# A four-layer kernel: softmax, sigmoid and one Silu written with Tanh, and a power by squarings on GpSimd

## The reference, cut to what matters

```
# conditioning of layer 1: each sequence has one expert of 8
expert = argmax(opcode_onehot, -1)
hidden = silu(x @ W_up[expert].T) * (x @ W_gate[expert].T)        # 256 wide
out = hidden @ W_down[expert].T

# feed-forward of layer 1: the two best of 8 experts for each token
gate_scores = softmax(x @ Wg + bg)                                # over 8 experts
topk_scores, topk_idx = top_k(gate_scores, 2)
top_probs = softmax(topk_scores)                                  # over the two
out = sum over the two of top_probs * (relu(x W1 + b1) W2 + b2)

# feed-forward of layer 2: again the two best of 8, routed by a sigmoid
probs = sigmoid(x @ router_w.T + routing_bias)
topk_p, topk_idx = top_k(probs, 2); topk_p /= sum(topk_p)
out = shared SwiGLU(x) + sum over the two of topk_p * (silu(x wg) * (x wu)) wd
```

## Time and profile before

| what | value |
|---|---|
| median of three runs | 1442.39 us (1441.62 to 1445.08) |
| the profiled execution | 1442.76 us, its span 1440.9 us |
| granted TensorE clock, mean of the span | 0.96 |
| PE, DVE, ACT, POOL busy | 1248.3, 856.1, 710.7, 269.1 us |
| instructions in the trace | 26352 |

### The profile page before, as it was taken

How to read it: one execution, slowest core, us unless ns; L and a number is a source line. 1 busy time by engine, 2 the same in 40 slices (tenths; PEclk the granted TensorE clock), 3 DMA queues, 4 the chain that set the end, 5 groups by cost and what they waited for, 6 DMA issues and landing times.

```text
span 1440.9 us, 26352 instructions
## 1 busy us (share of the span) xinstructions
PE 1248.3 (87%) x9301; PEld 967.7 (67%) x9301; DVE 856.1 (59%) x1800; ACT 710.7 (49%) x1385; POOL 269.1 (19%) x454
## 2 busy tenths in 40 slices
PE   4799960678988889998988999989999998998989
PEld 2455620346877779887777888589888854456867
DVE  4878669654445466657776445466564566664242
ACT  1556668545445434444444445333434376665554
POOL 1899200000001213330000003043320111100000
PEclk9899985799999999999999999999999999999999
DMA  8000010211050213212205200123120000000000
GB/s 304 1 2 2 2 73 0 116 81 59 1 198 10 90 56 102 56 29 96 110 1 210 88 1 25 48 80 88 36 94 1 1 1 2 2 2 1 0 15 15
DMA packets 42607, 75.71 MB, mean 53 GB/s; under 512 B 3817, under 2 KB 33521, under 8 KB 41585
## 3 DMA queue, kind: packets, MB, share of 16 engines
q1 hardware_dynamic: 38384, 65.62, 12.5%
q0 software_dynamic: 4096, 8.40, 2.0%
HBM read 59.72 MB, written 14.29 MB: 51 GB/s over the span
## 4 chain that ended last, share of the span: by engine, by line
PE 67%; DVE 15%; ACT 9%; issue 5%; POOL 2%; DVEq 1%; DMA 1%; ACTq 0%; SPq 0%; POOLq 0%
PE bank L1635 7%; PE bank L1624 7%; PE bank L1620 6%; PE bank L1679 5%; PE bank L1413 3%; PE bank L1479 3%; PE bank L1689 3%; PE bank L1611 3%; PE bank L1418 3%; PE bank L1420 2%; PE bank L1419 2%; PE bank L1604 2%; PE bank L1606 2%; PE bank L1605 2%; PE bank L1529 2%
## 5 line engine op out<-in xcount | busy, mean ns | idle before, releaser
L1872 ACT ACTIVATE SC<-bank 128x512 f32<-128x512 f32 x192 | 114.1, 596 | 220.4 <-PE bank L1620 130.3
L1959 DVE SCALAR_TENSOR_TENSOR SC<-bank,SM,SC 128x512 f32<-128x512 f32 x128 | 95.9, 749 | 142.6 <-PE bank L1624 119.7
L2549 POOL DMA_INDIRECT xs<-CC,POSI x64 | 63.6, 994 | 536.1 <-DVE POSI L2353 234.0
L1635 PE MATMUL bank<-A,SC 128*128 x1024 | 137.1, 277 | 10.5 <-DVE SC L1959 9.6
L1624 PE MATMUL bank<-X,SC 128*128 128x128 f32 x1024 | 137.3, 277 | 6.1 <-DVE SC L2234 5.8
L1620 PE MATMUL bank<-X,SC 128*128 128x128 f32 x1024 | 137.5, 278 | 2.0 <-ACT SC L1856 2.0
L1635 PEld LDWEIGHTS bank<-A,SC 128*128 128x128 f32 x1024 | 125.4, 192 | 20.2 <-issue 19.4
L1620 PEld LDWEIGHTS bank<-X,SC 128*128 128x128 f32 x1024 | 128.5, 195 | 14.4 <-issue 12.5
L1624 PEld LDWEIGHTS bank<-X,SC 128*128 128x128 f32 x1024 | 125.4, 193 | 8.2 <-DVE SC L2234 8.1
L1679 PE MATMUL bank<-A 128*128 128x128 f32 x736 | 99.6, 279 | 11.8 <-DVE A L2374 8.1
L1772 ACT ACTIVATE A<-bank,SM 128x128 f32<-128x128 f32 x256 | 73.6, 383 | 66.0 <-DVE SM L2055 65.7
(11 more groups left out here) (319 smaller groups left out, 2570.3 us busy)
## 6 DMA issues: line engine op xcount, KB each, us to landing
A<-in_moe SPq DMA_DIRECT2D x36, 768.0 KB, 10.2
A<-xs SPq DMA_DIRECT2D x20, 256.0 KB, 3.4
ys<-A SPq DMA_DIRECT2D x20, 256.0 KB, 2.4
BW<-in_l1f SPq DMA_DIRECT2D x2, 2048.0 KB, 7.8
BW<-in_l2f SPq DMA_DIRECT2D x1, 3456.0 KB, 12.0
BW<-in_l1c SPq DMA_DIRECT2D x1, 3072.0 KB, 17.0
BW<-in_l3f SPq DMA_DIRECT2D x1, 2816.0 KB, 9.5
A<-in_l1c SPq DMA_DIRECT2D x1, 2560.0 KB, 8.6
```

The source lines that it names most:

```text
L1635: m = e.matmul(o, at["h"].ap[:, cut(q)], W[:, bass.ds(r + (1024 + 128 * q), 128)], start=k == 0 and q == 0, stop=k == 1 and q == 3)
L1872: e.activation(at["h"].ap, at["pg"].ap, ACT.Gelu_apprx_tanh).then_inc(at["gelu"][0], 1)
L1959: return e.scalar_tensor_tensor(out=o, in0=a, scalar=s, in1=b, op0=o1, op1=o2)
```

## The change

The three functions are written with Tanh. For the conditioning, silu(u) * g = 0.5 * ((1 + tanh(u/2)) * u) * g: ACT does Tanh with scale 0.5, and DVE's one product becomes two that depend on each other, with a wait between them. For the routing, (1 + tanh(x/32)) / (1 - tanh(x/32)) is exp(x/16), and four squarings make exp(x) of it (for L = 1 exp(-x), so that 1 / (1 + it) is the sigmoid; the sign that DVE's form leaves is lost in the squarings). DVE makes the fraction with three instructions, POOL does the four squarings, and this is a step of its own, `r_pow`, and a stage of its own: `r_top` and `r_hot` come one round later than before. The weights of the two best, softmax over two, come of one Tanh and two independent instructions instead of Exp and three that wait for each other. For L = 1 `r_top` gets two instructions more.

```
@@ route_item: the semaphores and the stages
+                def s_pow():
+                    at = step("r_pow", prev=u["t"])
+                    at["x"] = [tick("ffn_vec") for _ in range(3)]
+                    at["sq"] = [tick("r_square") for _ in range(4)]
+                    u["t"] = at["sq"][3]
...
-                return ([(in_key, n)], [s_first, s0c, s0d], ("r", L, n))
+                return ([(in_key, n)], [s_first, s_pow, s0c, s0d], ("r", L, n))
@@ ACT
-                    e.activation(at["h"].ap, at["r"].ap[:, 0:256], ACT.Silu).then_inc(at["t"][0], 1)
+                    e.activation(at["h"].ap, at["r"].ap[:, 0:256], ACT.Tanh, scale=0.5).then_inc(at["t"][0], 1)
...
-                    e.activation(v4(RTT[0]), v4(RTT[0]), (ACT.Exp, ACT.Sigmoid)[at["L"]]).then_inc(at["t"][0], 1)
+                    e.activation(v4(RTT[0]), v4(RTT[0]), ACT.Tanh, scale=(1.0 / 32, -1.0 / 32)[at["L"]]).then_inc(at["t"][0], 1)
...
-                    e.activation(RT4[0], RT4[0], ACT.Exp).then_inc(at["e"][0], 1)
+                    e.activation(RT4[0], RT4[0], ACT.Tanh, scale=0.5).then_inc(at["e"][0], 1)
@@ DVE
-                    e.tensor_tensor(at["h"].ap, at["h"].ap, at["r"].ap[:, 256:512], ALU.mult).then_inc(at["t"][0], 1)
+                    stt(at["h"].ap, at["h"].ap, 1.0, at["r"].ap[:, 0:256], ALU.add, ALU.mult).then_inc(at["silu"][0], 1)
+                    w.wait_ge(*at["silu"])
+                    stt(at["h"].ap, at["h"].ap, 0.5, at["r"].ap[:, 256:512], ALU.mult, ALU.mult).then_inc(at["t"][0], 1)
...
+                elif kind == "r_pow":
+                    L_, x, R = v4(RTT[0]), at["x"], v4(RTT[4])
+                    w.wait_ge(*at["prev"])
+                    e.tensor_scalar(R, L_, 1.0, None, ALU.subtract).then_inc(x[0][0], 1)
+                    w.wait_ge(*x[0])
+                    e.reciprocal(R, R).then_inc(x[1][0], 1)
+                    w.wait_ge(*x[1])
+                    stt(L_, L_, 1.0, R, ALU.add, ALU.mult).then_inc(x[2][0], 1)
...
-                    if at["L"] == 0:
+                    if at["L"]:
+                        e.tensor_scalar(L_, L_, 1.0, None, ALU.add).then_inc(at["n"][0][0], 1)
+                        w.wait_ge(*at["n"][0])
+                        e.reciprocal(L_, L_).then_inc(at["n"][1][0], 1)
+                        w.wait_ge(*at["n"][1])
+                    else:
...
-                        e.tensor_scalar(s, d, 1.0, None, ALU.add).then_inc(at["w"][0][0], 1)
-                        w.wait_ge(*at["w"][0])
-                        e.reciprocal(P1, s).then_inc(at["w"][1][0], 1)
-                        w.wait_ge(*at["w"][1])
-                        e.tensor_tensor(P2, d, P1, ALU.mult).then_inc(at["w"][2][0], 1)
+                        ts(P1, d, -0.5, 0.5, ALU.mult, ALU.add)
+                        ts(P2, d, 0.5, 0.5, ALU.mult, ALU.add).then_inc(at["w"][0][0], 1)
@@ POOL
+                elif kind == "r_pow":
+                    L_, sq = v4(RTT[0]), at["sq"]
+                    w.wait_ge(*at["x"][2])
+                    for k in range(4):
+                        e.tensor_tensor(L_, L_, L_, ALU.mult).then_inc(sq[k][0], 1)
+                        if k < 3:
+                            w.wait_ge(*sq[k])
```

More of the change, by code:

```diff
@@ L697, in s0b @@
                     at = step("l1_gate", h=u["h"], r=u["r"], prev=u["t"])
+                    at["silu"] = tick("l1_vec")
                     at["t"] = u["t"] = tick("l1_vec")
@@ L943, in s0b @@
                     at["t"] = u["t"] = tick("ffn_act")
+                def s_pow():
[3 more added lines that the diff above has]
+                    u["t"] = at["sq"][3]
                 def s0c():
                     at = step("r_top", L=L, prev=u["t"])
-                    if L == 0:
-                        at["n"] = [tick("ffn_vec") for _ in range(3)]
+                    at["n"] = [tick("ffn_vec") for _ in range(3 if L == 0 else 2)]
                     at["top"], at["idx"], at["t"] = tick("ffn_vec"), tick("ffn_vec"), tick("ffn_vec")
@@ L956, in s0d @@
                     at = step("r_hot", L=L, n=n, prev=u["t"])
-                    at["w"] = [tick("ffn_vec") for _ in range(3)]
+                    at["w"] = [tick("ffn_vec") for _ in range(1 if L == 0 else 3)]
                     at["hot"] = sig["onehot", L, n] = tick("ffn_vec")
@@ L2298, in _ @@
                         e.tensor_tensor(P2, T8[:, :, 1], s, ALU.mult).then_inc(at["w"][2][0], 1)
-                    w.wait_ge(*at["w"][2])
+                    w.wait_ge(*at["w"][-1])
                     o5 = O_[h].rearrange("p (e k b) -> p k b e", e=8, k=2)
```

## The result

The changed kernel takes 1420.73 us (median of 4 runs, 1420.32 to 1420.98). Against the kernel before beside it (1443.74 us, median of 4 runs) the ratio is 0.984, with a 95% interval of 0.983 to 0.986: 23 us or 1.6% less. The forecast was 1419. In the profiles the span went from 1440.9 to 1418.9 us, 22.1 us less.

What follows compares the result with a forecast made beforehand. PE, busy 87% of the span, was taken as the bound, so only its waits counted. Gains of 13.8 + 2.3 + 0.9 + 0.9 + 5.9 = 23.8 us from 1442.76 gave 1419 us, range 1411 to 1426 (57%).

Steps and rivals of the forecast that it cites:

- Part 1: Routing, chunks 0 to 2 of both layers: table loads ahead of the gelu go, ending six PE waits; 13.8 us gained.
- Part 2: Loads around r_top of L = 0: PE's smaller waits of 5.33 us shrink to about 1.0 per chunk; 2.3 us gained.
- Part 3: Chunk 3, layer 2: the load ahead of L1916 goes and PE's 0.95 us wait with it; 0.9 us gained.
- rival E: No change: PE's waits have another cause behind the loads, and only the releaser changes; 3%.
- Part 4: Conditioning: two PE waits shrink by 3.5 us together, DVE's second product costs 2.6 us; net gain 0.9 us.
- Part 5: Work added to the routing, r_pow, squarings and r_top's extra instructions: hidden behind other work, costed at nothing.
- the cover: Chunk n = 1: 2.1 to 2.45 us before DVE reaches r_top, to hide POOL's squarings of 1.4 us.
- Part 6: Clock: three falls to 0.50 after routing waits go, 4.9 us, plus 1.0 us in the conditioning; 5.9 us gained.
- B: Rival: only table waits come back, clock falls move or are replaced, part 2 gives nothing; 1426 to 1432 us; 25%.
- C: Rival: more than forecast, part 2 giving 5.3, conditioning 3.5 and all clock falls going; 1406 to 1411 us; 12%.
- D: Rival, slower: DVE waits at r_top for POOL at eight places; decides when 8 x (4p - 2.45) = 24 us, p = 1.36 us per squaring; 3%.

Runs made afterwards that it cites:

- stage_only: Kernel before with only an empty stage between r_prob and r_top, all 51 table loads kept; 1449.36 us, ratio 1.004 to the kernel before.
- tanh_direct: Kernel before with Tanh put straight in for Exp and Sigmoid in the routing, no power, no extra stage, Silu kept; 1422.04 us, ratio 0.985 to before.
- late_again: Changed kernel with r_top's small Tanh (L = 0) moved on ACT into r_hot's step, one round later; 1418.60 us, ratio 0.982 to before.
- cond_only: Kernel before with only the conditioning changed: Tanh and two products for Silu and one; 1447.65 us, ratio 0.997 to before.
- logits_top: late_again, with L = 1's r_top on the logits and sigmoid of the two best only, no power, squarings or stage there; 1414.36 us, ratio 0.980 to before.
- square_dve: Changed kernel with the four squarings moved from POOL to DVE, behind r_pow's three instructions; 1426.79 us, ratio 0.982 to before.
- twelve: Changed kernel with twelve dependent POOL instructions instead of four in each r_pow; 1440.68 us, ratio 0.998 to before.
- eight: Changed kernel with eight dependent POOL instructions instead of four in each r_pow; 1424.65 us, ratio 0.987 to before.

## Why the prediction was right, and where it wasn't

**Part 1, 13.8 us, held.** The six waits sum to 14.4 us before, and 0.15 us is left: 14.3 us. stage_only and tanh_direct show that it is the loads.

**Part 2, 2.3 us, failed.** The step that failed is "I get about 1.0 us left for each chunk". 1.57, 1.54 and 1.75 us are left, 4.86 of 5.33 us, so that it gave 0.5 us. The table loads there had been covered in part by ACT's wait for DVE's chain; with the loads gone the wait is longer, 2.79 us in place of 1.34. late_again took the Tanh away from there and got back 3.4 us.

**Part 3, 0.9 us, gave nothing.** The row of PE's timeline after the change is

```profile
908.48 1.09 PE L1727 MATMUL bank<-SC,BW 128*128 128x512 f32 x2 [0.95 <-DVE SC L2475]
```

with the wait of the earlier trace rows to the hundredth, though the load ahead of L1922 is gone there. I had put down a wait to a load that stood near it in time, without a releaser that led to it. This is rival E in one place. The prediction also says that ACT is never idle ahead of a load. Here it was, for 0.48 us and PE's bank; only the first load of the program has an idle time before it too.

**Part 4, 0.9 us, was mis-sized low.** PE's idle time in the stretch fell by 1.4 us, and cond_only shows it is this part. The two waits on L1832 are gone, 5.2 us; the waits for DVE's products grew by 0.46 us each at the six places where they stood and appeared at two new places (0.36 and 0.41 us). PE's timeline of the changed kernel at the first of the new ones, the last row here:

```profile
302.25 0.33 PE L1558 MATMUL bank<-CC,A 128*128 128x128 f32 x1 [0.90 <-DVE A L1965]
...
305.93 0.47 PE L1558 MATMUL bank<-CC,A 128*128 128x128 f32 x1 [1.81 <-DVE A L1965]
...
307.82 0.48 PE L1558 MATMUL bank<-CC,A 128*128 128x128 f32 x1 [0.36 <-DVE A L1965]
```

**Part 5: the cover held, the sum of nothing did not.** A squaring takes 0.258 us in the mean, forecast 0.27, and four 1.18 to 1.32 us, forecast 1.4. The squarings' group in the changed kernel:

```profile
L2557 POOL TENSOR_TENSOR SM<-SM 128x32 f32<-128x32 f32 x32 | 8.3, 258 | 389.2 <-DVE SM L1965 387.3
```

`r_top` begins 1.12 us after their end in chunk 1, which with 1.32 is the forecast cover of 2.45 us. But I had worked it out for one chunk: in chunk 0 only 0.17 us was over. And what the part adds, said to be on no path, cost 2.3 to 2.5 us in layer 2; tanh_direct and logits_top both show it. Which piece of it costs is not shown by a run of its own: both kernels leave out the stage as well as DVE's added instructions, and stage_only, in which the loads are still there, lost 0.9 us in layer 2. square_dve adds 0.87 us to DVE for each chunk and lost only 0.2 us more there. That DVE's instructions are to blame rests on two rows alone: in chunk 2 PE's waits of 0.34 and 0.55 us are for DVE's copy and product, and the copy stands right behind `r_top`, which has the two added instructions. "DVE waits for the gelus" still holds at some places (0.87 us at 433.52) and not at these.

**Part 6, 5.9 us, held.** PE was busy at a granted clock of 0.50 for 2.9 us of layer 1's stretch and 6.6 us of layer 2's before, and for none of either now: at the full clock that is half, 4.8 us less, forecast 4.9. The busy times of the two stretches fell by as much, 2.9 and 1.9 us, though not divided as the falls are (1.5 and 3.3); why is open. In the conditioning it went from 14.3 to 11.2 us, 1.5 us less, forecast 1.0. PE's busy time in the whole span fell by 6.2 us in this profile, but by 9.1 in the second one, so that the whole span couldn't have borne it out to the microsecond. The falls of the clock at 477, 818 and 886 us are gone, here in windows of the same work:

```profile
467.00:470.00 3.00, 3.00 (x20) 2.35 (x20) 1.61 (x6) 1.62 (x3) 2.02 (x5) 1.00 0.95 328
804.00:807.00 3.00, 3.00 (x28) 3.00 (x29) 1.24 (x4) 1.78 (x4) 0.58 (x2) 1.00 0.00 0
867.00:870.00 3.00, 3.00 (x23) 2.52 (x23) 1.51 (x6) 1.91 (x4) 2.23 (x6) 1.00 0.07 22
```

Of the falls elsewhere some came and went without the edit (below).

**The sum.** The terms I missed are each small beside the whole: part 2 gave 1.8 us less, part 3 0.9 us less, part 5 cost 2.4 us, part 1 gave 0.5 and part 4 0.5 us more; that is 17.9 - 4.1 = 13.8 us. The three stretches measure 1.4 + 7.2 + 6.0 = 14.6 us less idle time of PE; about 1 us of part 5's cost is not idle but busy time (97.2 us in the change, 96.1 us in tanh_direct), so the two agree. With 1.2 us of waits elsewhere and 6.2 us of busy time it makes 22.0 us. So the forecast of 23.8 us met 22.1 with one term four fifths too high, a small one that gave nothing and one missing. That it lies so near is in part luck: the 1.2 us elsewhere were in no term, and they are less than two profiles of one program differ by.

**The rivals.** B, only the waits come back, didn't come: the clock did too. C, more than forecast, didn't either: part 2 gave 0.5 us where it had 5.3. D, DVE waits for POOL, is a true mechanism with the wrong point: with twelve instructions, each 0.32 us with its gap, the kernel is back at 0.998 of before. I had put the point at 4 x 1.36 = 5.4 us of POOL for each chunk; it lies near 3.8 us (397.86 to 401.70 us in chunk 0 of twelve). The waits themselves come nearly as the formula has them: 8 x (3.8 - 2.45) = 11 us, and DVE waits 12.1 us. But against the change the span is 20.2 us longer: PE's idle time is 16.2 us more (two profiles of the change differ by 2.8 in it), and its busy time 4.0 us more, where the clock fell. The formula counts neither the falls nor the rest of the idle time, and it set the waits against a gain of 24 us where 22 had come.

## What to carry to other kernels

Count a table load by the wait that it ends, not by the 1.28 us it takes: 27 loads of 34.6 us gave 14 us of waits at six places and 5 us at two (where DVE's second product took most of it back), and near nothing elsewhere. When a stall goes, look for the next instruction on the same in-order engine that waits for another one, and move it a round later; a single 0.2 us ACTIVATE that waits held 3.4 us. Work out a cover for each place where it is needed and not for one, and don't cost added work at nothing because the engine idles before the change.

## What the runs showed of the hardware

**POOL stands still for DVE's copy.** Of the four squarings of a chunk the one that starts while DVE's weight copy runs is longer, and it ends 0.09 us after the copy does. In the changed kernel's layer 2, chunk 0:

```profile
803.35 0.23 POOL L2557 TENSOR_TENSOR SM<-SM 128x32 f32<-128x32 f32 x1 [153.52 <-DVE SM L1965]
...
803.98 0.37 POOL L2557 TENSOR_TENSOR SM<-SM 128x32 f32<-128x32 f32 x1
```

DVE's copy beside them:

```profile
803.83 0.43 DVE L2242 COPY SC<-A 128x512 f32 x1 [0.56 <-issue]
```

0.23 us for the first, 0.37 us for the third, which starts within the copy of 803.83 to 804.26. Six of the eight chunks have such a squaring, of 0.30 to 0.37 us, and the chunks with no copy beside them have none; a product with one input in PE's accumulator beside a squaring left it at 0.24 us. The page "SBUF — State Buffer" of the Trainium skill, section "SBUF: two separate sides", has the shared pair of ports held for a whole instruction. For POOL the trace agrees, with a price of 0.13 us at most here. For DVE it isn't seen: the squaring before the long one, 803.66 to 803.90, is still running when the copy starts, and the copy takes 0.43 us, as it does with no squaring beside it.

**Added waits can cost twice their length.** In twelve's routing of layer 1, 5.4 us more of waits cost 11.2 us, since behind each wait of 3 to 4 us stand 3.3 to 6.6 us with a granted clock of 0.50. In the changed kernel none follows the waits of 1.5 to 1.8 us, and one follows a wait of 2.71 us; but in eight none follows one of 2.72 us, so the length of the wait doesn't settle it alone. What does was not tried.

**The falls of the clock aren't the same from run to run.** The first matmuls after 30 us took 2.04 and 1.91 us in one profile of the change and 1.10 and 1.05 us in the other, 1.9 us in all; a fall at 1137 us is in the second and not in the first. That moves a single profile by some 2 us in either direction with the program unchanged, and it is why the stretches and not the spans are compared above.
